# Values of the groups 2 to 7 from seven block products, dense weight sums from pairs of chunks

## What is computed

```python
x = conv_general_dilated(inputs, conv_w, ...) + conv_b      # 1024 -> 3 * 256
q, k, v = jnp.split(x, 3, axis=-1)                          # 256 each, in blocks of 128 tokens
vh = jnp.einsum('btd,dhe->bthe', v, wv) + bv                # 256 -> 16 heads of 64
scores = jnp.einsum('bqhe,bkhe->bhqk', qh * scale, kh)
p = jax.nn.softmax(jnp.where(causal, scores, NEG_INF))
o = jnp.einsum('bhqk,bkhe->bqhe', p, vh)
return (jnp.einsum('bqhe,hed->bqd', o, wo) + bo) @ proj_w + proj_b
...
y = jnp.einsum('bth,oh->bto', x, W_base) + b_base           # + experts weighted by a router
```

## Time and profile before

| | |
|---|---|
| median of 3 runs | 769.1 us (769.08 to 769.15) |
| the profiled execution | 769.19 us, span 767.4 us |
| TensorE busy | 749.3 us (98%), 5326 matmuls |
| VectorE busy | 552.6 us (72%) |
| ScalarE busy | 452.5 us (59%) |
| GpSimd busy | 173.2 us (23%) |
| mean granted clock of TensorE | 0.998 of full speed |

### The profile page before, as it was taken

The page is one execution under the profiler, slowest core; times in us unless marked ns, Lnnn a source line. Parts: engine busy times, 40 slices in busy tenths (PEclk is TensorE's granted clock), DMA queues, the critical chain, the costliest instruction groups (busy, mean ns, idle before and its releaser), DMA issues.

```text
span 767.4 us, 15056 instructions
## 1 busy us (share of the span) xinstructions
PE 749.3 (98%) x5326; PEld 673.8 (88%) x5326; DVE 552.6 (72%) x1503; ACT 452.5 (59%) x1180; POOL 173.2 (23%) x204
## 2 busy tenths in 40 slices
PE   4999999999999999999999999999999999999997
PEld 3898888888888888999898999999989899999997
DVE  6999996879888875656556555456588567777774
ACT  5963433334433788687777787777794155566530
POOL 2300100000000124525162626252430201222200
PEclk9999999999999999999999999999999999999999
DMA  8846833444445345442525160702057976333402
GB/s 326 297 118 192 255 121 125 172 164 145 163 151 206 111 167 144 146 174 72 195 71 186 37 227 18 232 1 111 1 195 221 364 216 204 133 121 137 160 29 83
DMA packets 61246, 118.86 MB, mean 155 GB/s; under 512 B 11507, under 2 KB 30067, under 8 KB 59892
## 3 DMA queue, kind: packets, MB, share of 16 engines
q1 hardware_dynamic: 59156, 110.56, 43.0%
q0 software_dynamic: 2016, 7.34, 2.3%
HBM read 82.68 MB, written 34.80 MB: 153 GB/s over the span
## 4 chain that ended last, share of the span: by engine, by line
PE 92%; DVE 3%; ACT 2%; issue 1%; DMA 1%; DVEq 0%; POOL 0%; ACTq 0%; POOLq 0%
PE net_psum L63 15%; PE net_psum L65 15%; PE net_psum L64 15%; PE net_psum L1791 11%; PE net_psum L2033 5%; PE net_psum L2035 5%; PE net_psum L2034 5%; PE net_psum L1853 4%; PE net_psum L1864 4%; PE net_psum L1876 4%; PE net_psum L1906 2%; PE net_psum L1907 2%; PE net_psum L1908 2%; PE net_psum L1775 1%; ACT pr L888 1%
## 5 line engine op out<-in xcount | busy, mean ns | idle before, releaser
L719 POOL TENSOR_TENSOR pr<-pr,rrec 128x512 f32<-128x512 f32 x64 | 66.5, 1040 | 209.2 <-DVE rrec L1328 206.0
L888 ACT ACTIVATE pr<-pr,negmax 128x128 f32<-128x128 f32 x256 | 99.0, 395 | 1.0 <-DVE negmax L1320 1.0
L1791 PE MATMUL net_psum<-ua,wa 128*128 128x256 f32 x384 | 83.8, 379 | 0.6 <-DVE ua L1210 0.6
L1791 PEld LDWEIGHTS net_psum<-ua,wa 128*128 128x128 f32 x384 | 72.6, 190 | 10.4 <-issue 0.8
L1320 DVE CUSTOM_DVE_ANT_0 pr<-net_psum,mask 128x128 f32<-128x128 f32 x256 | 57.0, 286 | 29.6 <-PE net_psum L1853 29.6
L63 PE MATMUL net_psum<-x_hi,w_hi 128*128 128x512 f32 x192 | 76.4, 398 | 0.0
L64 PE MATMUL net_psum<-x_lo,w_hi 128*128 128x512 f32 x192 | 76.2, 397 | 0.0
L845 ACT ACTIVATE w_hi<-raw 128x1024 fp32r<-128x1024 f32 x24 | 25.5, 1062 | 85.5 <-PE net_psum L65 76.8
L65 PE MATMUL net_psum<-x_hi,w_lo 128*128 128x512 f32 x192 | 75.6, 393 | 0.0
L63 PE MATMUL net_psum<-c_hi,wqk_hi 128*128 128x256 f32 x256 | 74.1, 290 | 0.0
L64 PE MATMUL net_psum<-c_lo,wqk_hi 128*128 128x256 f32 x256 | 71.6, 280 | 0.0
(11 more groups left out here) (268 smaller groups left out, 2257.4 us busy)
## 6 DMA issues: line engine op xcount, KB each, us to landing
wa<-in_conv_w SPq DMA_DIRECT2D x24, 512.0 KB, 4.2
raw<-in_conv_w SPq DMA_DIRECT2D x24, 384.0 KB, 4.2
xn<-in_x SPq DMA_DIRECT2D x16, 512.0 KB, 10.2
xr<-in_x SPq DMA_DIRECT2D x8, 1024.0 KB, 5.6
x_scratch<-xr SPq DMA_DIRECT2D x8, 1024.0 KB, 4.4
x1t<-x_scratch SPq DMA_DIRECT2D x16, 512.0 KB, 5.1
x1g<-x_scratch SPq DMA_DIRECT2D x56, 128.0 KB, 3.0
out<-x1t POOLq DMA_DIRECT2D x14, 512.0 KB, 3.0
```

The source lines that it names most:

```text
L719: pool.tensor_tensor(pr[:, jj % 4], pr[:, jj % 4], rrec[:, jj % 4].unsqueeze(2).to_broadcast([P, UN, P]), ALU.mult).then_inc(s["p_ready"], 1)
L888: e = act.activation(pr[:, jj % 4, un], pr[:, jj % 4, un], ACT.Exp, bias=negmax[:, jj % 2, un:un + 1], scale=-1.0, accum_out=rsum[:, jj % ...
L1791: mm = pe.matmul(duo_acc(d, mi)[:, v * QUADS:(v + 1) * QUADS], wa[:, a % AW, mi, 1 - v, c % 2], ua[:, c, v, n * QUADS:(n + 1) * QUADS], st ...
```

## The change

**Seven products.** For the groups from `SEVEN` = 2 on, a group's values are a product of 2 x 2 blocks: A is the group's `c` (token block i, channel chunk j; 128 x 128), B the value weights (channel chunk i, column half j; 128 x 512). Eight block products, 24 matmuls, become seven, 21 matmuls, with these sums: S1 = A21 + A22, S2 = S1 - A11, S3 = A11 - A21, S4 = A12 - S2, T1 = B12 - B11, T2 = B22 - T1, T3 = B22 - B12, and B21 - T2. The products go in the order A11 B11, A12 B21 | S2 T2 | S1 T1, S3 T3 | S4 B22, A22 (B21 - T2), where a bar divides the units (the first two units are slot q = 1, the others q = 2). Most of them are added to what stands in one of the two banks, and after each the bank is read out or added to `vf` by VectorE (`value_out`), the third by a copy on ScalarE. The head outputs of the group's first pair wait for all seven reads.

**The sums of the weights** are made once, from `wv_again`, the value weights loaded a second time: four subtractions on VectorE (`value_weight_sums`) at the end of slot 5, ahead of `pw_lo`; three copies `vt_hi` on ScalarE at the end of its slot 5, ahead of `pw_hi`, which wait for these; three subtractions `vt_lo` on VectorE at the end of slot 6, ahead of `pw_lo`; one copy into `wv_hi` in slot 6 and one subtraction (`low_last_sum`) in slot 7. **The sums of c** are made for each group: four additions of 128x128 on VectorE in slot q = 3 of the group before, their high part `vs_hi` on ScalarE, and the low part `vs_lo` at the end of slot q = 0.

**Dense weights.** Since `wv_again`, `vt_hi` and the others need room, `fw_raw` is loaded late: for the sums only two chunks at a time stand in `w_pair`, and `gate_weights(n)` puts the experts' columns in for each pair (behind slots 7, 11, 15 and 19) and for the chunks of the dense layer itself (slots 25 and 31). Its first four chunks are loaded behind the last sum, its last four when the values of all groups are done.

```diff
+    SEVEN = 2
+    V_SUMS = WC + 4
+
+    def v_before(e):
+
+        return VT * min(e, SEVEN) + 7 * max(0, e - SEVEN)
...
+            def load_weights(*rows):
+                for to, c in rows:
+                    for (lo, hi), off, (left, right) in zip(COLS, OFF, OUT):
+                        sync.dma_start(to[:, lo + off:lo + off + right - left], w_base[:, c, left:right]).then_inc(s["fw_loaded"], 16)
...
+                    sync.dma_start(wv_again[:], wv).then_inc(s["wv_loaded"], 16)
...
-                    for c in range(DC):
-                        for (lo, hi), off, (left, right) in zip(COLS, OFF, OUT):
-                            sync.dma_start(fw_raw[:, row(c), lo + off:lo + off + right - left], w_base[:, c, left:right]).then_inc(s["fw_loaded"], 16)
+                    load_weights(*((w_pair[:, row(c) // 4], c) for c in (0, 4)))
+                if 1 < g <= TSUMS // 4 and i == 5:
+                    sync.wait_ge(s["t_step"], sum_step(4 * (g - 1) - 1))
+                    load_weights(*((w_pair[:, row(c) // 4], c) for c in (g - 1, g + 3)))
+                if (g, i) == (TSUMS // 4 + 1, 6):
+                    sync.wait_ge(s["t_step"], sum_step(TSUMS - 1))
+                    load_weights(*((fw_raw[:, row(c)], c) for c in range(4)))
                 if (g, i) == (8, 0):
+                    sync.wait_ge(s["v_done"], v_before(NG))
+                    load_weights(*((fw_raw[:, row(c)], c) for c in range(4, DC)))
```

On ScalarE:

```diff
+                if q == 2 and SEVEN <= g < NG:
+                    act.wait_ge(s["o_done"], 2 * (D - PV) + 2)
+                    act.wait_ge(s["v_ready"], v_before(g) + 2)
+                    act.wait_ge(s["v_done"], v_before(g) + 3)
+                    act.activation(vf[:, 0, BANK:2 * BANK], vy[0], ACT.Copy).then_inc(s["v_ready"], 1)
...
+                if D == 5:
+                    act.wait_ge(s["v_low_step"], V_SUMS)
+                    for i, block in enumerate((value_block(0, 0), value_block(1, 1), value_block(0, 1))):
+                        act.activation(vt_hi[:, i], block, ACT.Copy).then_inc(s["v_high_ready"], 1)
+                if D == 6:
+                    act.wait_ge(s["v_done"], v_before(SEVEN))
+                    act.activation(wv_hi[:, 0, BANK:2 * BANK], value_block(1, 0), ACT.Copy).then_inc(s["v_high_ready"], 1)
+                if q == 3 and SEVEN <= g + 1 < NG:
+                    act.wait_ge(s["v_low_step"], v_low(g + 1) + 4)
+                    act.activation(vs_hi[:], vs_raw[:], ACT.Copy).then_inc(s["v_high_ready"], 1)
```

On VectorE:

```diff
+            def value_out(e, step, i, j, bank):
+
+                to = vf[:, i, j * BANK:(j + 1) * BANK]
+                dve.wait_ge(s["v_done"], v_before(e) + step)
+                if step == 4:
+                    dve.wait_ge(s["v_ready"], v_before(e) + 3)
+                if step in (1, 4, 7):
+                    dve.tensor_copy(to, vy[bank]).then_inc(s["v_ready"], 1)
+                else:
+                    dve.wait_ge(s["v_ready"], v_before(e) + step - 1)
+                    dve.tensor_tensor(to, vy[bank], to, ALU.add).then_inc(s["v_ready"], 1)
...
+            def value_weight_sums():
+
+                b11, b12, b21, b22 = value_block(0, 0), value_block(0, 1), value_block(1, 0), value_block(1, 1)
+                dve.wait_ge(s["wv_loaded"], 32)
+                for k, (to, left, right) in enumerate(((b11, b12, b11), (b12, b22, b12), (b22, b22, b11), (b21, b21, b22))):
+                    dve.wait_ge(s["v_low_step"], WC + k)
+                    dve.tensor_tensor(to, left, right, ALU.subtract).then_inc(s["v_low_step"], 1)
...
+            def low_value_sums():
+
+                for i, block in enumerate((value_block(0, 0), value_block(1, 1), value_block(0, 1))):
+                    dve.wait_ge(s["v_high_ready"], WC + i + 1)
+                    dve.tensor_tensor(vt_lo[:, i], block, vt_hi[:, i], ALU.subtract).then_inc(s["v_low_step"], 1)
...
+            def low_last_sum():
+
+                dve.wait_ge(s["v_high_ready"], WC + 4)
+                dve.tensor_tensor(wv_lo[:, 0, BANK:2 * BANK], value_block(1, 0), wv_hi[:, 0, BANK:2 * BANK], ALU.subtract).then_inc(s["v_low_step"], 1)
...
+                dve.wait_ge(s["c_loaded"], 16 * e)
+                dve.tensor_tensor(s1, a21, a22, ALU.add).then_inc(s["v_low_step"], 1)
+                dve.tensor_tensor(s3, a11, a21, ALU.subtract).then_inc(s["v_low_step"], 1)
+                dve.wait_ge(s["v_low_step"], v_low(e) + 1)
+                dve.tensor_tensor(s2, s1, a11, ALU.subtract).then_inc(s["v_low_step"], 1)
+                dve.wait_ge(s["v_low_step"], v_low(e) + 3)
+                dve.tensor_tensor(s4, a12, s2, ALU.subtract).then_inc(s["v_low_step"], 1)
...
+            def low_values(e):
+
+                dve.wait_ge(s["v_high_ready"], WC + 4 + e - SEVEN + 1)
+                dve.tensor_tensor(vs_lo[:], vs_raw[:], vs_hi[:], ALU.subtract).then_inc(s["v_low_step"], 1)
...
-                if is_v:
+                if is_v and e >= SEVEN:
+                    if D % DG == 1 and k == 0:
+                        value_out(e, 1, 0, 0, 0)
+                        value_out(e, 2, 0, 0, 1)
+                    elif D % DG == 2 and k == 0:
+                        value_out(e, 4, 1, 1, 1)
+                        value_out(e, 5, 1, 1, 0)
+                    elif D % DG == 2:
+                        value_out(e, 6, 0, 1, 1)
+                        value_out(e, 7, 1, 0, 0)
+                elif is_v:
...
+                if D == 7:
+                    low_last_sum()
+                if q == 3 and SEVEN <= g + 1 < NG:
+                    value_sums(g + 1)
...
-                if D == TFIRST - 1:
-                    gate_weights()
                 weight_sums(D, True)
+                if TFIRST - 1 <= D < sum_at(TSUMS) - 1 and q == 3:
+                    gate_weights((D + 1 - TFIRST) // DG)
+                if D == W_LAST:
+                    gate_weights(TSUMS // 4)
+                if D == ND - 1:
+                    gate_weights(TSUMS // 4 + 1)
+                if D == 5:
+                    value_weight_sums()
+                if D == 6:
+                    low_value_sums()
+                if q == 0 and SEVEN <= g < NG:
+                    low_values(g)
```

The dense weights:

```diff
+            def gate_weights(n):
+
+                pair = n < TSUMS // 4
+                dve.wait_ge(s["fw_loaded"], 16 * NB * (2 * n + 2 if pair else 2 * TSUMS // 4 + (4 if n == TSUMS // 4 else DC)))
+                if n == 0:
+                    dve.wait_ge(s["az_loaded"], 64 * E_ACT)
+                for rows, chunks in (((w_pair, slice(row(n) % 4, row(n) % 4 + 5, 4)),) if pair else
+                                     ((fw_raw[:, 6:8], slice(6, 8)), (fw_raw[:, 0:2], slice(0, 2))) if n == TSUMS // 4 else
+                                     ((fw_raw[:, 2:6], slice(2, 6)),)):
+                    dve.memset(rows[:, :, 3 * QW - PAD:3 * QW + PAD], 0.0)
+                    half, two = ER // 2, E_ACT // 2
+                    for h in range(2):
+                        dve.tensor_copy(rows[:, :, QW * h:QW * h + half], a_raw[:, chunks, half * h:half * h + half])
+                        z = dve.tensor_copy(rows[:, :, QW * h + half:QW * h + ZW], r_raw[:, two * h:two * h + two, chunks].rearrange("p e c -> p c e"))
                 z.then_inc(s["t_step"], 1)
...
-                b11, b12 = fw_raw[:, row(c), 0:2 * QW], fw_raw[:, row(c), 2 * QW:WZ]
-                b21, b22 = fw_raw[:, row(c + 4), 0:2 * QW], fw_raw[:, row(c + 4), 2 * QW:WZ]
+                b11, b12 = w_pair[:, row(c) // 4, 0:2 * QW], w_pair[:, row(c) // 4, 2 * QW:WZ]
+                b21, b22 = w_pair[:, row(c + 4) // 4, 0:2 * QW], w_pair[:, row(c + 4) // 4, 2 * QW:WZ]
```

On TensorE:

```diff
+            def value_product(bank, x_hi, x_lo, w_hi, w_lo, first):
+
+                pe.matmul(vy[bank], x_hi, w_hi, start=first, stop=False, skip_group_check=True)
+                pe.matmul(vy[bank], x_hi, w_lo, start=False, stop=False, skip_group_check=True)
+                pe.matmul(vy[bank], x_lo, w_hi, start=False, stop=True, skip_group_check=True).then_inc(s["v_done"], 1)
...
+            def seven_values(D, k, e):
+
+                at = v_before(e)
+                c = lambda i, j: (c_block(c_hi[e % 2], i, j), c_block(c_lo[:, e % 2], i, j))
+                b = lambda i, j: (wv_hi[:, i, j * BANK:(j + 1) * BANK], wv_lo[:, i, j * BANK:(j + 1) * BANK])
+                sums = lambda i: (vs_hi[:, i], vs_lo[:, i])
+                weights = lambda i: (vt_hi[:, i], vt_lo[:, i])
+                if D % DG == 1 and k == 0:
+                    emptied(pe, D, 0)
+                    value_product(0, *c(0, 0), *b(0, 0), True)
+                    emptied(pe, D, 1)
+                    pe.wait_ge(s["pT_ready"], min(2 * (D - TR + 1), NJ))
+                    value_product(1, *c(0, 1), *b(1, 0), True)
+                elif D % DG == 1:
+                    pe.wait_ge(s["v_ready"], at + 1)
+                    pe.wait_ge(s["v_low_step"], v_low(e) + 5)
```

(18 more changed lines are left out.)

70 lines of the change are left out of this document (49 added, 21 removed).

## The result

The changed kernel takes 780.44 us (median of 4 runs, 780.41 to 780.49) against 769.1: a ratio of 1.0147 (95% interval 1.013 to 1.0165), slower by 11.3 us. Forecast were 780.0, between 771 and 784.

What follows compares the result with a forecast made beforehand. TensorE, with work in 98% of the span, was taken as the bound. Onto 769.1 came stalls 2.5 + 7.6, clock 1.5, less 0.7 gained: +10.9, 780.0 us; range 771 to 784, the forecast's own 776.5 to 784.

Steps and rivals of the forecast that it cites:

- Gain 0: Slots q = 1: groups 2 to 6 gain nothing from three fewer matmuls, as TensorE waits for kf; group 7 gains 0.7.
- My own test: Prediction wrong if the vt_lo run in a row, or if slots 9, 13, 17, 21 and 25 get shorter.
- The steady costs: Each group's added reads and sums, and late dense loads at the end: put at 0, bounds 1.2 and 1.5.
- The stall of slot 6: TensorE waits 2.5 us for kf, delayed by ScalarE waiting for VectorE's four subtractions; bounds 1.7 and 3.
- The stall of slot 7: VectorE's vt_lo and pw_lo delay a_lo and TensorE's first projection: 7.6 us (1.0 + 6.6), bounds 1.0 and 8.6.
- The turns: In slot 7 VectorE and GpSimd alternate, one whole instruction each, when both queues are full: 6.6 us more for VectorE.
- The clock: TensorE may run at its lower clock after idling in slot 7: 1.5 us taken, bounds 0 and 5.5.
- the first: Rival: VectorE's queue keeps the port for its four instructions in slot 7, no turns: 771.9 us, chance 0.16.
- the second: Rival: setup costs nothing at first and each of six groups gains its three matmuls: 764.9 us, chance 0.06.
- third: Rival: no change, subtractions cost one microsecond of stall only against a gain of 0.7: 769.4 us, chance 0.06.
- the fourth: Rival: slot 7's stall goes on through slot 8, late loads or steady slots: 785 us or more, chance 0.06.

Runs made afterwards that it cites:

- three_out: The kernel before, with only the last three matmuls of the second value product left out in groups 2 to 7 (result incomplete): 768.47 us, ratio 0.9989.
- three_out_chi_late: The kernel before, with those three matmuls per group left out and the c_hi copies of slots q = 1 behind the last kf (result incomplete): 763.54 us.
- dense_pairs: Only the dense part of the change (paired and late weight loads), values from eight products, no sums: 769.08 us against 769.12 for the kernel before.
- both_early: The changed kernel, four weight subtractions moved ahead of VectorE's read in slot 5, three vt_lo ahead of its read in slot 6: 769.17 us.
- chi_late_after: The changed kernel, four subtractions and three vt_lo ahead of VectorE's reads in slots 5 and 6, c_hi copies behind the last kf of slots q = 1: 764.83 us.
- lows_early: The changed kernel, with only the three vt_lo subtractions moved ahead of VectorE's read of unit k = 0 in slot 6: 772.31 us.
- filled_stall: The changed kernel, with 20 unused matmuls of 512 columns ahead of the first projection product of slot 7: 779.33 us.
- filled_whole: The changed kernel, with 28 unused matmuls of 512 columns ahead of the first projection product of slot 7: 778.05 us.
- bias_early: The changed kernel, with GpSimd's two bias sums for group 0 moved from slot 7 to slot 5: 773.85 us.
- sums_early: The changed kernel, with only VectorE's four value-weight subtractions moved ahead of its read of unit k = 0 in slot 5: 777.39 us.

## Why the prediction was right

**The groups.** "Gain 0" for groups 2 to 6 and 0.7 for group 7 hold: -0.72 and +0.67 to +0.78, and -0.71. The score rows are 2.10, as forecast. `three_out` against `three_out_chi_late` show the cause: ScalarE's kf behind c_hi. My own test for it was badly drawn, though: I wrote that slots 9, 13, ... would be as long as before and that I was wrong if they got shorter. A slot starts with its first score matmul, so the 0.7 is taken off slot 9 and put on slot 10. Only the sum of the two tells. So by the letter of my own test I was wrong there, and the mechanism held all the same.

**The steady costs** (at 0): right. `dense_pairs` and `both_early` leave nothing to find but some 0.3 in slot 8. They are small only while kf is late, though: in `chi_late_after` slot 22 is 0.7 and slot 8 0.4 longer than in `three_out_chi_late`, and that is the 1.1 us between the two.

**The stall of slot 6.** Forecast 2.5 (1.7 to 3), measured 2.17. The mechanism was the one named. What was missed is a term: I put a clock loss behind the long stall alone, and 2.2 us of waiting was followed by 1.7 of half clock too. In other executions (`lows_early` with 2.12, `filled_stall` with 2.11, `filled_whole` with 2.17) the wait was followed by none; what decides it isn't shown.

**The stall of slot 7.** Forecast 7.6, measured 5.19. The turns are right, instruction by instruction; `bias_early` takes them away (1.08 is left of 8.04). The size failed at the step "they start where pw_lo does now, 302.99, plus the 2.5". VectorE starts them behind its last read of slot 6, which waits for TensorE and so carried the half clock too: 306.66, 3.67 later than pw_lo before. GpSimd's c_lo stands behind a multiply that waits for VectorE's reciprocal, and this for ScalarE's exponentials; it was only 2.30 later, 305.68. So c_lo was already under way, VectorE waited for 0.86 of it instead of all, and pw_lo no longer had a bias sum ahead of it. `sums_early`, with slot 6 undisturbed, shows the order of the forecast and 6.39, so that the order is 1.2 of the 2.4 that were missed. Of the other 1.2 the sum overlooked two pieces of room in the kernel before. VectorE's timeline there, first mask of slot 7:

```profile
304.87 0.29 DVE L1320 CUSTOM_DVE_ANT_0 pr<-net_psum,mask 128x128 f32<-128x128 f32 x1 [0.37 <-PE net_psum L1853]
```

VectorE sat idle for 0.37 there, and pw_lo's 1.51 held 0.3 of waiting already (1.21 in the changed kernel). The remaining 0.5 isn't taken apart.

**The clock.** Forecast 1.5, measured 1.7 + 2.9 = 4.6. The bounds I gave, 0 and 5.5, held it; the value was chosen without a row. For the long stall, the only one it was meant for, it is 1.5 against 2.9. `filled_whole` shows that there the idling was the cause.

**The sum.** Stalls 2.7 less than forecast, clock 3.1 more: 780.0 against 780.4 is right to 0.4 only because two sizes were off against each other. The steps and their places hold, two of the four terms don't. The forecast's own range, 776.5 to 784, isn't the sum of my bounds either: with turns these give 777.7 (no clock lost, 1.7 in slot 6) to 785.5.

The rivals: the first (VectorE keeps the port, 771.9) fell with the vt_lo rows, the second and third with slots 6 and 7, the fourth with the slots behind, where nothing changed but the exchange of 0.7 within each group.

The Trainium skill (SBUF — State Buffer, Who interferes with whom) says that such a pair of instructions locks the other out for its whole length; the rows at 306 to 313 us agree (vt_lo 2.85 instead of 0.63).
